# Turning normalised x by DMA transposes of f16 row splits, a third weight buffer, and another order of ScalarE's work in the first chunk

## The reference, cut to what matters

```python
xn = _layernorm(x, axis=-1)
s = _L0_attn_ref(xn, W_Q, W_K, W_V, W_O, b_Q, b_K, b_V, b_O)
# _L0_ffn_ref: out = ((silu(xn @ gate_w.T * gate_s) * (xn @ up_w.T * up_s)) @ down_w.T) * down_s
g = _silu(_L0_ffn_ref(xn, gate_w, up_w, down_w, gate_s, up_s, down_s))
x = x + s * g
```

## Time and profile before

| | us |
|---|---|
| three runs | 1144.65, 1145.84, 1147.0 (median 1145.84) |
| the profiled execution, device time | 1144.51 |
| its span | 1143.2 |
| TensorE busy | 1121.1 (98%) |
| VectorE busy | 674.4 (59%) |
| ScalarE busy | 581.4 (51%) |
| GpSimd busy | 84.6 (7%) |
| mean granted TensorE clock | 0.998 of 2.4 GHz |

### The profile page before, as it was taken

One profiled execution on the slowest core, in us unless ns is written; L12 is line 12 of the kernel. 1 busy time (PEld: TensorE's weight loads), 2 busy tenths in 40 slices (PEclk: granted clock), 3 DMA queues, 4 the chain that ended last, 5 costly groups with the idle time before them and its releaser, 6 DMA issues.

```text
span 1143.2 us, 23441 instructions
## 1 busy us (share of the span) xinstructions
PE 1121.1 (98%) x5772; PEld 546.9 (48%) x5772; DVE 674.4 (59%) x1523; ACT 581.4 (51%) x1276; POOL 84.6 (7%) x104
## 2 busy tenths in 40 slices
PE   5999999999999999999999999999999999999998
PEld 3344444444544454454444445445444444445444
DVE  6665354445665556656655555665665555666775
ACT  5854253334665555555555555555555454544452
POOL 1000000002100000000000000000000000134364
PEclk9999999999999999999999999999999999999999
DMA  6411111112454333333344433334334633357546
GB/s 229 169 37 37 41 61 47 64 46 62 103 90 97 78 78 78 85 80 78 78 86 88 88 80 78 78 80 85 78 78 85 122 60 70 64 125 190 132 96 161
DMA packets 236756, 101.77 MB, mean 89 GB/s; under 512 B 219456, under 2 KB 219456, under 8 KB 236736
## 3 DMA queue, kind: packets, MB, share of 16 engines
q1 hardware_dynamic: 231200, 85.78, 34.5%
q0 software_dynamic: 3424, 11.54, 3.2%
q10 hardware_dynamic: 2112, 4.19, 1.0%
HBM read 38.57 MB, written 8.39 MB: 41 GB/s over the span
## 4 chain that ended last, share of the span: by engine, by line
PE 94%; DMA 2%; DVE 1%; ACT 1%; issue 1%; SPq 0%; DVEq 0%; ACTq 0%
PE bank L436 85%; PE bank L589 9%; DMA arena<-arena 1%; PE bank L449 1%; DMA arena<-ffn_w_dram 1%; DMA arena<-x_dram 0%; DVE arena L888 0%; ACT arena L837 0%; ACT arena L824 0%; DVE arena L1143 0%; SPq L335 0%; ACT lo_abs L714 0%; DVE arena L1076 0%; DVE stats L906 0%; DVE arena L1147 0%
## 5 line engine op out<-in xcount | busy, mean ns | idle before, releaser
L436 PE MATMUL bank<-XT_hi,arena 128*128 (+1 forms) x1392 | 453.4, 380 | 2.0 <-issue 1.9
L436 PE MATMUL bank<-XT_lo,arena 128*128 (+1 forms) x864 | 328.1, 380 | 0.0
L436 PE MATMUL bank<-arena 128*128 (+1 forms) x1124 | 268.2, 380 | 0.1
L436 PEld LDWEIGHTS bank<-XT_hi,arena 128*128 (+1 forms) x1392 | 136.4, 98 | 161.2 <-issue 6.3
L824 ACT ACTIVATE arena<-bank,neg_max 128x512 f32<-128x512 f32 (+3 forms) x256 | 132.6, 524 | 133.8 <-DVE neg_max L1060 133.7
L436 PEld LDWEIGHTS bank<-arena 128*128 (+1 forms) x1124 | 107.6, 98 | 124.7 <-issue 11.5
L436 PE MATMUL bank<-arena,XT_hi 128*128 (+1 forms) x512 | 152.3, 379 | 0.0
L1076 DVE SCALAR_TENSOR_TENSOR arena<-arena,inv_sum 128x512 f16<-128x512 f32 (+3 forms) x256 | 145.5, 629 | 4.2 <-ACT arena L837 3.8
L436 PEld LDWEIGHTS bank<-XT_lo,arena 128*128 (+1 forms) x864 | 84.8, 98 | 92.6 <-issue 0.8
L837 ACT ACTIVATE arena<-arena,inv_sum 128x512 f16<-128x512 f32 (+3 forms) x256 | 122.4, 558 | 0.8 <-DVE inv_sum L1068 0.8
L1060 DVE CUSTOM_DVE_ANT_0 bank<-bank,mask 128x512 f32<-128x512 f32 (+3 forms) x256 | 117.5, 520 | 0.5 <-PE bank L436 0.5
(11 more groups left out here) (82 smaller groups left out, 1047.7 us busy)
## 6 DMA issues: line engine op xcount, KB each, us to landing
w_in<-attn_w_dram SPq DMA_DIRECT2D x64, 256.0 KB, 2.6
arena<-ffn_w_dram SPq DMA_DIRECT2D x11, 768.0 KB, 4.5
arena<-x_dram SPq DMA_DIRECT2D x16, 256.0 KB, 3.6
parked_silu<-arena ACTq DMA_DIRECT2D x4, 1024.0 KB, 4.5
arena<-x_dram POOLq DMA_DIRECT2D x12, 256.0 KB, 2.9
arena<-parked_silu POOLq DMA_DIRECT2D x12, 256.0 KB, 3.1
out_dram<-arena POOLq DMA_DIRECT2D x12, 256.0 KB, 2.8
arena<-arena SPq DMA_TRANSPOSE x128, 4.2
```

What stands on the lines that cost most here:

```text
L436: mm = nc.tensor.matmul(out, stationary(a, k), moving(b, k), start=first and n == 0 and i == 0, stop=last and n == len(tiles) - 1 and i == ...
```

## The change

- The chunks 1 to 3 are no longer transposed by TensorE. Of each normalised 128-row tile ScalarE makes the hi part as rows (`split_rows`, `XS[0]`) and VectorE the lo part (`XS[1]`), and SyncE turns each of the two with a DMA transpose of 4 blocks of 128x128 straight into XT_hi and XT_lo (`turn_rows`): 8 DMA transposes per chunk, 24 in all. A chunk's first gate product waits for all 8 to have landed (`xt_turned`). Chunk 0 is turned as before.
- XS and a third buffer for FFN weights lie in the memory of V, which nothing else uses before the attention.
- `load_x(c + 1)` stands behind the transposes of chunk c in SyncE's queue. The transposes of chunk 3 stand between the loads of the attention's weight slices 4 to 7. ffn tile 2 is loaded at the head of the program, ahead of the last two of the three constant loads.
- For the chunks 1 to 3 GpSimd computes 1/sqrt(var + eps) as a power of -0.5 on 128x4 values; ScalarE's root and its two table switches stay for chunk 0 alone.
- In chunk 0 the three lists go. ScalarE splits tile m+3 and sums tile m+2 **between** silu and `ht_hi` of step m, and at m = 7 and 8 also copies two rows of chunk 1 there. VectorE splits three tiles before step 0 and then tile m+3 behind step m; its maximum over tile 1 comes behind step 0; the statistics of chunk 1 come one row tile per step (m = 2 to 5), its scaling at m = 6 and 7, its row splits at m = 7 and 8.

The core of the diff:

```diff
-AHEAD = [(2, 3), (4, 5), (6,), (7,), (8,), (9,), (10,), (), (), ()]
-SUMMED_BEHIND = [(2,), (), (5,), (6,), (7,), (8,), (9,), (), (10,), ()]
+FB = 3
...
+            def load_ffn(m):
+                if m >= FB:
+                    sp.wait_ge(fw_lo, 3 * (m - FB + 1))
+                sp.dma_start(FFN_IN[m % FB], ffn_w[m]).then_inc(ffn_loaded[m % FB], 16)
...
+            def turn_rows(c, tiles=range(TT)):
+                for t in tiles:
+                    for part, split in ((0, xs_hi), (1, xs_lo)):
+                        sp.wait_ge(split, TT * (c - 1) + t + 1)
+                        sp.dma_start_transpose(out=XT[part][:, :, c * S + t * P:c * S + (t + 1) * P],
+                                               in_=XS[part][:, t]).then_inc(xt_turned, 16)
+            for c in range(1, B - 1):
+                turn_rows(c)
+                load_x(c + 1)
...
+            for c in range(1, B):
+                pool.wait_ge(var_ok, c + 1)
+                nc.gpsimd.tensor_tensor(rstd0[:], var_eps[:], minus_half[:], ALU.pow).then_inc(std_ok, 1)
...
-                    pe.wait_ge(xt_lo, KT * (c + 1))
+                    pe.wait_ge(xt_turned, 16 * 2 * TT * c)
...
-                    for k in range(2):
-                        transpose_x(c + 1, k)
-                    steps(c, 6, 10, exact)
-                    for k in range(2, KT):
-                        transpose_x(c + 1, k)
...
+            def split_rows(c, tiles):
+                if c > 1 and tiles[0] == 0:
+                    act.wait_ge(xt_turned, 16 * 2 * TT * (c - 1))
+                for t in tiles:
+                    act.wait_ge(xn_ok, TT * c + t + 1)
+                    nc.scalar.activation(XS[0][:, t], x_in[:, t], ACT.Copy).then_inc(xs_hi, 1)
...
+            def first_chunk(m):
+                if m + 3 < MT:
+                    split_ffn(m + 3)
+                if m + 2 < MT:
+                    sum_lo(m + 2)
+                if m in (7, 8):
+                    split_rows(1, (0, 1) if m == 7 else (2, 3))
+            for m in range(1, MT - 1):
+                step(0, m, m % 2, amid=lambda: first_chunk(m))
...
+                if m + 3 < MT:
+                    split_ffn(m + 3)
+                if 2 <= m < 2 + TT:
+                    token_stats(1, (m - 2,))
+                if m == 5:
+                    variances(1)
+                if m in (6, 7):
+                    scale_x(1, (0, 1) if m == 6 else (2, 3))
+                if m in (7, 8):
+                    split_rows(1, (0, 1) if m == 7 else (2, 3))
```

More of the change, by code:

```diff
@@ L153, in build @@
         XT = [sb(f"XT_{n}", [P, KT, T], F16) for n in ("hi", "lo")]
-        V = [sb(f"V_{n}", [P, 2, TT, HG * E], F16) for n in ("hi", "lo")]
+        v_hi_lo = sb("V", [P, 2 * 2 * TT * HG * E], F16)
+        V = [v_hi_lo[:].rearrange("p (s b t n) -> p s b t n", s=2, b=2, t=TT)[:, part] for part in (0, 1)]
+        XS = [v_hi_lo[:, part * TT * D:(part + 1) * TT * D].rearrange("p (t d) -> p t d", t=TT) for part in (0, 1)]
+        third = v_hi_lo[:, 2 * TT * D:2 * TT * D + 2 * 3 * 512].bitcast(F32)
+        FFN_IN = [part.rearrange("p (w n) -> p w n", w=3) for part in (ffn_in[:, :3 * 512], ffn_in[:, 3 * 512:], third)]
         Q = [sb(f"Q_{n}", [P, S], F16) for n in ("hi", "lo")]
@@ L192, in v_bank, with xt_bank @@
             return SC[0] if isinstance(t, int) and t == 1 else VB
-        def xt_bank(c, k):
-            return bank[2 + k] if isinstance(c, int) and c == 0 else XB[k % 2]
+        def xt_bank(k):
+            return bank[2 + k]
         const_loaded = sem("const_loaded")
@@ L212, in build @@
         xt_lo = sem("xt_lo")
-        ffn_loaded = [sem("ffn_loaded0"), sem("ffn_loaded1")]
+        xs_hi = sem("xs_hi")
+        xs_lo = sem("xs_lo")
+        xt_turned = sem("xt_turned")
+        ffn_loaded = [sem(f"ffn_loaded{i}") for i in range(FB)]
         fw_hi = sem("fw_hi")
@@ L439, in product, with transpose_x @@
                 return mm
[L442 to L445, removed]
+            def transpose_x(k):
                 for t in range(TT):
                     if k == 0:
-                        pe.wait_ge(xn_ok, TT * c + t + 1)
-                    tr = nc.tensor.transpose(to[:, t * P:(t + 1) * P], x_in[:, t, k * P:(k + 1) * P], ident[:])
+                        pe.wait_ge(xn_ok, t + 1)
+                    tr = nc.tensor.transpose(xt_bank(k)[:, t * P:(t + 1) * P], x_in[:, t, k * P:(k + 1) * P], ident[:])
                 tr.then_inc(xt_mm, 1)
@@ L490, in steps, with begin_chunk @@
                         step(c, 2 * i + par, par, (c, 2 * i + par - 1, 1 - par), exact, split_weights)
-            def begin_chunk(c, exact, transposes=None):
-                step(c - 1, MT - 1, 2, (c - 1, MT - 2, 1), exact, False, transposes)
+            def begin_chunk(c, exact):
+                step(c - 1, MT - 1, 2, (c - 1, MT - 2, 1), exact)
                 step(c, 0, 0, (c - 1, MT - 1, 2), exact)
-            def transpose_rest():
-                for k in range(2, KT):
-                    transpose_x(1, k)
             def later_chunks(exact):
-                begin_chunk(1, exact, transpose_rest)
+                begin_chunk(1, exact)
                 with pe.Fori(1, B - 1) as c:
                     step(c, 1, 1, (c, 0, 0), exact)
-                    steps(c, 2, 6, exact)
-                    for k in range(2):
-                        transpose_x(c + 1, k)
-                    steps(c, 6, 10, exact)
-                    for k in range(2, KT):
-                        transpose_x(c + 1, k)
+                    steps(c, 2, 10, exact)
                     begin_chunk(c + 1, exact)
@@ L528, in _ @@
             for k in range(KT):
[L529 removed]
+                transpose_x(k)
             pe.wait_ge(fw_lo, 1)
@@ L736, in park, with step @@
                 act.dma_start(parked_chunks[c], ffn_out).then_inc(park_done, 16)
-            def step(c, m, slot, down_of=None, x_of=None):
+            def step(c, m, slot, down_of=None, amid=None):
                 n = MT * c + m
```

163 lines of the change are left out of this document (69 added, 94 removed).

## The result

| | before | with the change |
|---|---|---|
| median of 5 runs, us | 1146.65 (1144.65 to 1147.0) | 1140.05 (1137.98 to 1141.08) |
| profiled execution, us | 1144.51, span 1143.2 | 1138.34, span 1136.8 |

The ratio is 0.9944, with a 95% interval of 0.9933 to 0.9955: 6.6 us less at the medians and 6.4 us less in the spans of the profiled executions. (Two more runs of the kernel before bring its median from 1145.84 to 1146.65.) The forecast was 1138.5, 7.3 us less, in a range of 1134 to 1143.

The account below looks back on a forecast made before the run. TensorE, busy for 1121.1 of 1143.2 us, was taken to bound the kernel. The terms -5.2 - 3.8 - 2.2 + 3.9 gave -7.3 us, from a median of 1145.84 to 1138.5, in a range of 1134 to 1143.

Parts of the forecast that it names:

- The transposes, -5.2: Chunks 1 to 3: 48 of 64 transposes leave TensorE's path at 0.109 us each, 5.2 us less.
- The wait at the first check, -3.8: Chunk 0, check of tile 2: TensorE's 2.1 us wait and the low clock behind it go, 3.8 us less.
- The gaps between steps, -2.2 and +3.45: Chunk 0, checks of tiles 3 to 10: old late-flag gaps go, 2.2 us; new waits come, largest 1.8 ahead of step 9.
- The head, +0.45: Program start: later constants make step 0's `ht_lo` 0.15 us late and the first branch 0.3 us late.
- Rival 1: Chunk 0's new waits, chiefly the 1.8 us: the clock falls, costing 1.7 us, 1140.2; chance 0.25.
- Rivals 2 and 5: 2: GpSimd's power late once, about 1141, chance 0.08. 5: tile 3 or 2 still lands late, 1141.5, chance 0.05.
- Rival 3: Chunk 0: added waits do not show since VectorE's and ScalarE's rows overlap more, -11.2, 1134.6; chance 0.12.
- Rival 4: Chunk 1's start: DMA transposes go one after the other, done 16 us late, +9.3, 1155; chance 0.05.
- point of decision: Rival 4 decides from 2.85 us per transpose in the queue, where chunk 1's gate product waits 7.2 us.
- The attention, 0: Attention: same code in both kernels and bounded by TensorE, so no difference expected.

Follow-up runs that it names:

- the ballast: Changed kernel with 48 dummy TensorE transposes put back, 8 at each of the six old places; 1144.09 us, ratio 0.9989.
- the swap: Kernel before with ScalarE's sum of weight tile 2 put ahead of its split of tile 3, nothing else; 1145.32 us, ratio 0.9992.
- the run again: The changed kernel run again with no edit, for a second profile and five more times; 1138.97 us, ratio 0.9936.
- flag_first: Changed kernel, chunk 0: VectorE's check right behind each weight split, chunk 1's row splits behind step 8, hi parts turned before lo; 1137.48 us, ratio 0.992.

## Why the prediction was right, and where its terms were off

- **The transposes, -5.2.** Right, and shown by the stretch behind chunk 0 (-5.1) and by the ballast (+5.1). Taking 0.109 us from the piece of 8 in the chain and not the row's mean of 312 ns decided it; the latter would have given 15 us.
- **The wait at the first check, -3.8.** Its size was about right: the wait and the low clock are gone, the clock is 1.00 over 24 to 32. The step that failed is the sentence "Its reason is ScalarE's order". Swapping the two in ScalarE's order gained 0.6 us of 1146, which is nothing, and the new order without the third buffer cost 6.7. What the runs show in its place is a load that can't start before a buffer is free (27.78 with the swap, 16.12 with two buffers). The number came out because the change brings both; that was luck as far as the reason goes.
- **The gaps between steps, -2.2 and +3.45.** Right in sum (3.4 above the ideal now), and largely in place: 0.33 ahead of step 7 (0.6 forecast), 0.36 ahead of step 8 (0.45), 0.25 at `ht_lo` of step 7 (0.5), 1.5 ahead of step 9 (1.8). The smaller ones were each somewhat less, and steps 4 and 6 lost 0.15 and 0.11 that I had in the sum as 0.1 for steps 2 to 4.
- **The head, +0.45.** Here the sum missed: the first branch showed 0.51 us (0.3 forecast) and the check of tile 2 came at 26.59, where 26.3 + 0.15 was expected. That this is near is chance: TensorE did not wait for `ht_lo` of step 0 at all in this execution, but started 0.2 us later than before (its first wait is 9.7 us instead of 9.5). In the run again the constants landed later still, and it cost 1.1 us at `ht_lo` of step 0 where 0.15 stood. I had taken the constants' delay from the loads' mean rate, but their landing varied by 0.8 us between two executions (13.8 and 14.63).
- **Rival 1, the clock in the new waits** (0.25). Not seen: 1.00 over 68 to 72 us with 1.5 us of standing in it. The Trainium skill (TensorE: Matmul & The Clock Gate, A second HAM failure mode) says that frequent short idle spells between groups of matmuls can be enough. The 1.5 us here were not; in this case's traces the clock fell behind waits of 1.9 us and more, and not behind each of those.
- **Rivals 2 and 5.** The power was 3.2 us early, and no load of weights was late.
- **Rival 3, no new waits.** It did not happen, but flag_first, the variant that makes the flag first, shows how: the rows need not overlap, they need only stand behind the flag.
- **Rival 4, the transposes in sequence.** Mechanism and place as described when forced, with the late landing as worked out (7 x 2.4 + 8.6 - 21.4 = 4.0, measured 4.1). Its point of decision, 2.85 us, was too high, since it left out the clock: 2.4 us already take the whole gain. (Its 16 us at 3.8 to 4.2 us each are 13.8 to 16.6 by the same sum.)
- **The attention, 0.** The code's time did not change, but its one wait for a DMA differs by 0.4 us and sometimes by its clock; that noise accounts for 0.4 of the 0.9 us between forecast and measurement, the head and first branch for the rest.

## What to carry to other kernels

An order and the buffer that permits it are one change: with two buffers, a swap in the old order gave nothing and the new order cost 6.7 us. A flag that a branch reads belongs ahead of all work that TensorE does not wait for, 1.5 us or more before the branch is due. A cost per instruction is read from a piece of the chain, and what the chain of the moved work collides with next is looked for before it is moved.

## What the runs showed of the hardware that was not expected

- Issuing a DMA transpose costs SyncE's queue 1.19 to 1.30 us for 4 blocks. I had 1.5 for 13 blocks, and 4 blocks were not a third of that, though they land in 2.4 to 3.1 us (median 2.5) instead of 3.8 and more. The last seven of chunk 1 start 1.3 us apart, and over 72 to 76 us the DMA share is 0.50: the queue's issue, not the engines' work (0.7 us each by my estimate), sets their pace.
- What standing does to the clock: 1.5 us ahead of step 9 left it at 1.00, and so did the 2.0 us at the first branch of the swap's run (1.00 over 28 to 32). 1.9 us in the attention dropped it to 0.64 in one execution, and 2.3 us at the same place left it at 1.00 over the next window in another. With the flag first the same wait of 2.3 us was followed by 0.86 and 0.72. After 3.2, 4.1 and 4.4 us it was 0.73, 0.50 and 0.62 over four us. So near 2 us it can go either way in two executions of one program.
- From the flag's write to the first matmul behind the branch there are 1.3 to 1.5 us (1.30 before, 1.38 with the change, 1.52 with two buffers), of which TensorE's queue shows nothing but "issue".
